# Attention scores of four heads side by side in 32-row tiles instead of stacked key rows

## The reference

```python
q = (query @ Wq.T).reshape(B, L, H, D) * scale      # L = 256, H = 16, D = 32
k = (key @ Wk.T).reshape(B, -1, H, D)               # key = value = ctx_1024, 25088 x 512
v = (value @ Wv.T).reshape(B, -1, H, D)
scores = jax.nn.sigmoid(jnp.einsum('blhd,bshd->bhls', q, k))
o = jnp.einsum('bhls,bshd->blhd', scores, v).reshape(B, L, E)
return o @ Wo.T
```

## Time and profile before

| | us |
|---|---|
| median of three executions | 2024.05 |
| the profiled execution | 2024.77 |
| its span, first to last instruction | 2023.1 |
| TensorE matmul busy | 1986.1 (98%) |
| TensorE weight load busy | 1777.9 (88%) |
| VectorE busy | 1225.8 (61%) |
| ScalarE busy | 1006.7 (50%) |

### The profile page before, as it was taken

One profiled execution on the slowest core, in us unless ns is written; L12 is line 12 of the kernel. 1 busy time (PEld: TensorE's weight loads), 2 busy tenths in 40 slices (PEclk: granted clock), 3 DMA queues, 4 the chain that ended last, 5 costly groups with the idle time before them and its releaser, 6 DMA issues. The chain is left out here.

```text
span 2023.1 us, 50717 instructions
## 1 busy us (share of the span) xinstructions
PE 1986.1 (98%) x19340; PEld 1777.9 (88%) x19340; DVE 1225.8 (61%) x2116; ACT 1006.7 (50%) x1129; POOL 26.8 (1%) x31
## 2 busy tenths in 40 slices
PE   7999999999999999999999999999999999988999
PEld 6888999888899988889998888999888899756998
DVE  6666566666656666665666666566666656335322
ACT  3445555454555545455554545555454555533764
POOL 4000000000000000000000000000000000000000
PEclk9999999999999999999999999999999999999999
DMA  5555655555565555556555555555555554543784
GB/s 189 132 155 151 161 136 153 144 143 150 150 161 136 153 144 143 150 150 161 136 154 143 143 150 150 161 136 153 144 143 150 150 151 107 132 160 127 270 286 160
DMA packets 127938, 311.95 MB, mean 154 GB/s; under 512 B 33720, under 2 KB 33720, under 8 KB 108856
## 3 DMA queue, kind: packets, MB, share of 16 engines
q1 hardware_dynamic: 95784, 215.93, 41.1%
q10 hardware_dynamic: 32112, 95.43, 15.0%
HBM read 155.52 MB, written 1.57 MB: 78 GB/s over the span
## 5 line engine op out<-in xcount | busy, mean ns | idle before, releaser
L346 ACT ACTIVATE probs<-sc 128x1024 f32<-128x1024 f32 x784 | 760.7, 1023 | 793.2 <-PE sc L647 786.7
L613 PE MATMUL kp<-x_combos,weights_r 128*128 128x256 f32 x4116 | 552.7, 284 | 8.2 <-DVE x_combos L448 3.5
L613 PEld LDWEIGHTS kp<-x_combos,weights_r 128*128 128x128 f32 x4116 | 521.1, 193 | 9.1 <-DVE x_combos L448 3.7
L632 PE MATMUL vp<-more_weights,x_combos 128*128 128x256 f32 x3528 | 472.7, 284 | 3.6 <-DVE v L497 3.6
L647 PE MATMUL sc<-rows_r,k_stack_r 96*128 96x256 f32 x3136 | 452.2, 287 | 2.8 <-ACT probs L346 2.8
L632 PEld LDWEIGHTS vp<-more_weights,x_combos 128*128 128x128 f32 x3528 | 446.1, 193 | 3.7 <-issue 3.7
L647 PEld LDWEIGHTS sc<-rows_r,k_stack_r 96*128 96x128 f32 x3136 | 404.0, 192 | 45.2 <-issue 40.7
L662 PE MATMUL acc<-probs,v 128*32 128x256 f32 x6272 | 360.6, 382 | 0.1
L476 DVE TENSOR_TENSOR k_parts<-k_parts,kp 128x512 f32<-128x512 f32 x245 | 168.2, 687 | 306.7 <-PE kp L613 306.7
L662 PEld LDWEIGHTS acc<-probs,v 128*32 128x32 f32 x6272 | 194.3, 110 | 131.7 <-issue 1.4
L448 DVE TENSOR_TENSOR x_combos<-ctx_raw,x_combos 128x512 fp32r<-128x512 f32 x240 | 169.2, 705 | 8.1
(11 more groups left out here) (145 smaller groups left out, 958.3 us busy)
## 6 DMA issues: line engine op xcount, KB each, us to landing
k_stack_r<-k_rows_hi SPq DMA_DIRECT2D x784, 64.0 KB, 2.3
k_stack_r<-k_rows_lo SPq DMA_DIRECT2D x784, 64.0 KB, 2.0
k_stack_r<-k_stack_r SPq DMA_DIRECT2D x196, 256.0 KB, 3.0
ctx_raw<-ctxT_dram ACTq DMA_DIRECT2D x47, 1024.0 KB, 5.7
piece<-w_all_dram ACTq DMA_DIRECT2D x176, 256.0 KB, 5.0
w_raw<-w_all_dram SPq DMA_DIRECT2D x44, 1024.0 KB, 4.8
weights<-wqk_dram SPq DMA_DIRECT2D x2, 1024.0 KB, 11.6
rows_r<-q_rows SPq DMA_DIRECT2D x3, 512.0 KB, 7.6
```

The source lines that it names most:

```text
L346: nc.scalar.activation(probs[:, t % 2, g, :], sc[g % 2][:], ACT.Sigmoid).then_inc(probs_ready, 1)
L613: last = nc.tensor.matmul(k2[:, r, :], wk[i - 1][:, k, a, r * P:(r + 1) * P], xc[:, i - 1, k, b, :], start=i in FRESH and n == 0, stop=n = ...
L632: last = nc.tensor.matmul(v2[:, r, :], xc[:, i - 1, k, b, r * P:(r + 1) * P], wv_c[i - 1][:, k, a, :], start=i in FRESH and n == 0, stop=n ...
```

## The change

The stacks, `stack_rows` and all key DMAs go. The projected rows are written to `k_rows`, which has two parities (chunks) of four quadrants, hi and lo. `scores` now reads them where they lie: head j has partitions 32j to 32j + 31, so each matmul uses 32 rows of the array, and the four heads of a group use four different row strips. The three terms hi·hi, hi·lo, lo·hi, once done by stacking, are now three accumulating matmuls. A call makes two groups: 2 groups × 3 terms × 4 heads = 24 matmuls of 32 rows × 128 columns against 256 query columns, where 8 matmuls of 96 rows stood. Each head writes to its own PSUM bank, so the score tile `sc_heads` takes the place of both `sc` tiles: it holds two groups, and there is one of it. One sigmoid reads all of it (2048 elements a partition, once instead of twice 1024), and the next pair waits for that sigmoid. The order of pairs over tiles and groups changes with it. The loads of the context and of the scanned pieces move from ScalarE's queue to SyncE's. The queries need no stack either; at the start their two trips through memory go. In TensorE's written order, K4 and V4 are parted, and V4 to V7 and P3 to P7 trade places:
P0 K1 V1 P1 K2 V2 P2 K3 V3 K4 P3 W01 P4 V4 K5 P5 V5 K6 P6 V6 K7 V7 P7 W23.

```diff
-        kst, kst_f32 = keep["two_types"](stack, "k_stack", [P, 2, 2, HG, 2, HS])
+        k_rows, k_rows_f32 = keep["two_types"](stack, "k_rows", [P, 2, 4, 2, 2, HS])
-        kr_hi, kr_lo = sb("k_rows_hi", [P, 2, 2, HS], F32R), sb("k_rows_lo", [P, 2, 2, HS], F32R)
-        sc = [stack.enter_context(nc.psum_tensor(f"sc{i}", [P, HG * L], F32)) for i in range(2)]
+        sc_heads = stack.enter_context(nc.psum_tensor("sc", [P, HG, 2, L], F32))
...
+        BY_HALF = [(t, g) for half, groups in enumerate(((0, 2), (2, 0))) for g in groups for t in (2 * half, 2 * half + 1)]
+        BY_TILE = [(t, g) for t in range(TC) for g in (0, 2)]
+        PAIRS = len(BY_HALF)
+        AT_HALF = {(0, 0): 0, (0, 2): 1, (1, 2): 2, (1, 0): 3}
...
-            for q in range(4):
-                stack_rows(0, q)
...
             def sigmoid(c, n, at, first):
...
-                nc.scalar.activation(probs[:, t % 2, g, :], sc[g % 2][:], ACT.Sigmoid).then_inc(probs_ready, 1)
+                nc.scalar.activation(probs[:, t % 2, g:g + 2, :].rearrange("p h (j l) -> p h j l", j=HG),
+                                     sc_heads[:, :, :, :].rearrange("p j h l -> p h j l"),
+                                     ACT.Sigmoid).then_inc(probs_ready, 1)
...
                 if i >= 5:
                     dve.wait_ge(k_sum, m * 5 + (i - 2))
-                    at = q % 2
-                    if q == 2:
-                        dve.wait_ge(hi_moved[0], m * MOVED + MOVED)
-                        dve.wait_ge(lo_moved[0], m * MOVED + MOVED)
...
-                    nc.vector.tensor_copy(kr_hi[:, at, :, :], to).then_inc(k_hi, 1)
+                    nc.vector.tensor_copy(k_rows[:, par, q, 0, :, :], to).then_inc(k_hi, 1)
...
-            def scores(c, n, order, free):
+            def scores(c, par, n, order, free):
                 t, g = order[n]
+                half = t // 2
                 if free:
-                    pe.wait_ge(probs_ready, c * (TC * G) + (n - 1))
...
-                for j in range(HG):
-                    last = nc.tensor.matmul(sc[g % 2][:, j * L:(j + 1) * L],
-                                            kst[0:3 * D, t // 2, g // 2, j, g % 2, t % 2 * P:(t % 2 + 1) * P],
-                                            qst[0:3 * D, j, g, :], start=True, stop=True)
+                    pe.wait_ge(probs_ready, c * PAIRS + n)
+                q = AT_HALF[half, g]
+                if q == 0:
+                    pe.wait_ge(k11_lo, c + 1)
+                else:
+                    pe.wait_ge(k_lo, c * 3 + q)
+                for r in range(2):
+                    for k_part, q_part in ((0, 0), (0, 1), (1, 0)):
+                        for j in range(HG):
+                            rows = slice(D * j, D * (j + 1))
+                            last = nc.tensor.matmul(sc_heads[:, j, r, :],
+                                                    k_rows[rows, par, q, k_part, r, t % 2 * P:(t % 2 + 1) * P],
+                                                    q_rows[q_part][rows, g + r, :], start=(k_part, q_part) == (0, 0),
+                                                    stop=k_part == 1)
                 last.then_inc(scores_ready, 1)
...
                 pair(2)
                 keys(3)
                 v_product(m, 3)
+                keys(4)
                 pair(3)
-                keys(4)
-                v_product(m, 4)
                 weigh(c, par, 0, BY_HALF)
                 weigh(c, par, 1, BY_HALF)
                 pair(4)
+                v_product(m, 4)
                 keys(5)
+                pair(5)
                 v_product(m, 5)
-                pair(5)
                 keys(6)
+                pair(6)
                 v_product(m, 6)
-                pair(6)
                 keys(7)
+                v_product(m, 7)
                 pair(7)
-                v_product(m, 7)
                 weigh(c, par, 2, BY_HALF)
```

More of the change, by code:

```diff
@@ L269, in _, with scan_piece @@
-            sp.dma_start(f32(qst[2 * D:3 * D, :, :, :]), kept_q[1]).then_inc(q_stacked, 16)
-            for q in range(4):
-                stack_rows(0, q)
             sp.dma_start(x1[:], x_rows).then_inc(x_loaded, 16)
             def one(c, par, first, k_next, split_next, looped):
[L274 to L278, removed]
+                def scan_piece(t):
+                    sp.wait_ge(piece_used, c * TC + (t - t % 2 - TC + 1))
+                    sp.dma_start(piece[:, t % 2, :], w_all[c - 1][:, t * PIECE:(t + 1) * PIECE].bitcast(I32)
+                                 ).then_inc(piece_loaded[t % 2], 16)
@@ L280, in _ @@
+                if looped:
+                    scan_piece(0)
+                    scan_piece(1)
+                if split_next:
+                    sp.wait_ge(x_ready, c * 7 + 14)
+                    sp.dma_start(raw[:], ctxT[c + 2]).then_inc(ctx_loaded, 16)
+                if looped:
+                    scan_piece(2)
+                    scan_piece(3)
             chunks(sp, one)
@@ L390, in _ @@
                 elif i == 4:
-                    k_first(0, first=True)
+                    k_first(0, 0)
                     v_first(0, 0)
@@ L464, in wk_rest, with k_first_rest, k_summed @@
                                         f32(wk[i - 1][:, :, 0, :]), ALU.subtract).then_inc(wk_ready, 1)
-            def k_first_rest(m, first=False):
+            def k_first_rest(m, par):
                 dve.wait_ge(k11_hi, m + 1)
-                if not first:
-                    dve.wait_ge(lo_moved[2], m * MOVED)
-                nc.vector.tensor_tensor(kr_lo[:, 0, :, :], k2, f32(kr_hi[:, 0, :, :]), ALU.subtract).then_inc(k11_lo, 1)
-            def k_summed(m, i, first=False):
+                nc.vector.tensor_tensor(k_rows[:, par, 0, 1, :, :], k2, f32(k_rows[:, par, 0, 0, :, :]),
+                                        ALU.subtract).then_inc(k11_lo, 1)
+            def k_summed(m, par, i):
                 add, q = SUMS[i]
@@ L657, in weigh @@
                     pe.wait_ge(v_sum, c * 5 + 5)
-                for n, g in ((n, g) for n, (tile, g) in enumerate(order) if tile == t):
-                    pe.wait_ge(probs_ready, c * (TC * G) + (n + 1))
+                for n, g in ((n, g + r) for n, (tile, g) in enumerate(order) if tile == t for r in range(2)):
+                    pe.wait_ge(probs_ready, c * PAIRS + (n + 1))
                     for j in range(HG):
@@ L678, in pair @@
                 def pair(p):
-                    for n in (2 * p, 2 * p + 1):
-                        scores(c, n, BY_HALF if k_next else BY_TILE, not (first and p == 0))
+                    scores(c, par, p, BY_HALF if k_next else BY_TILE, not (first and p == 0))
                 def keys(i):
```

82 lines of the change are left out of this document (24 added, 58 removed).

## The result

The changed kernel takes 2460.89 us in the median of four executions (2457.36 to 2464.48), against 2024.12 for the kernel before: ratio 1.216, 95% interval 1.214 to 1.218. It is 437 us slower. The forecast was 2275, with a range up to 2335. The sign was right; the size was off by 186 us.

What follows compares the result with a forecast made beforehand. The prediction took TensorE's own program as the bound. Its sum: 2024.8 + 189 + 9 (chunks 0, 45, 46) + 0.6 (chunk 47) + 59 (clock) - 10 (start) + 3 (end) = 2275 us, range 2200 to 2335.

Steps and rivals of the forecast that it cites:

- Step 1: Score block on TensorE: 24 matmuls on four strips take 0.76 us where 0.96 stood, -1.6 us a chunk.
- Step 2: Mode changes around TensorE's score blocks: 0.18 us each, +2.2 us a chunk.
- Step 3: TensorE waits 3.7 us at K6 in each looped chunk for VectorE's read of K5: +189 us over 44 chunks.
- Step 4: TensorE's clock falls after each K6 wait, costing 1.3 us in a looped chunk: +59 us in all.
- Step 5: Kernel's start without key DMA waits: -10 us; last chunk with a single score tile: +3 us.
- Step 6: Key DMAs, the loop's sigmoids and SyncE's queue: costed at nothing.

Runs made afterwards that it cites:

- e3: Changed kernel with VectorE's combinations ahead of V4's sum and TensorE's 44 looped chunks written out without a loop: 2037.92 us, ratio 1.007 to the kernel before.
- e9: e1 with its loop kept, but score blocks leave out the lo-keys term, 16 matmuls instead of 24: 2068.17 us, ratio 1.022 to the kernel before.
- e7: e2 with TensorE's blocks in the whole order of the kernel before: 2080.11 us.
- e6: e2 with V4 moved back ahead of the weighing in TensorE's order, only K6 between P5 and P6: 2063.94 us.
- e5: e2 with 15 matmuls of zeros ahead of K6, keeping TensorE busy through the wait: 2214.42 us, ratio 1.094 to the kernel before.
- e1: Changed kernel, loop kept, with VectorE's three combinations and first two scans ahead of V4's sum: 2212.89 us, ratio 1.093 to the kernel before.
- e11: e2 with V4 ahead of the weighing and a K and a V product ahead of each pair from P5 on: 2038.75 us.
- e2: Changed kernel with TensorE's 44 looped chunks written out, other engines' loops kept: 2279.61 us, ratio 1.126 to the kernel before.
- e4: Kernel before, with four chunks instead of two in TensorE's loop body: 2098.71 us, ratio 1.037 to the kernel before.
- e8: e3 with a score block's loops of terms and heads exchanged, so three matmuls in a row use one 32-row strip: 2042.7 us.
- e12: e3 with heads outermost in a score block, so all six matmuls of a head follow each other: 2448.6 us.

## Why the prediction was wrong, step by step

- **Step 1, the score block, right.** 0.76 us forecast from first to last start and stagger. Read from e3, 1212.09 to 1213.00 is 0.91 with the change of mode, 0.18: 0.73. Four strips run side by side in fp32r as in f32, at 0.12 a round; e9, with two rounds less, has chunks 1.86 us shorter, 0.116 a round.
- **Step 2, the changes of mode, right.** 0.18 each by the rows before, 0.18 by e7 against e6. Steps 1 and 2 together were to make the chunk 0.6 us longer; it is 0.31 longer. Over 48 chunks the difference is 14 us, the largest error among the terms that stood in the sum.
- **Step 3, the wait at K6, right in place, cause and size.** 3.7 us forecast, 3.47 to 3.6 of idle time in the profile, 3.7 by e5 against e3, and e1 and e11 lift it from either side.
- **Step 4, the clock, right.** 1.3 us for each wait forecast, 1.4 by e5 (1.5 in a looped chunk). The choice of 1.3 over 2.6 leaned on a misread row: in the 8 us before K1 TensorE had done V7 and P0, not one score block alone. That 1.3 came out was in part luck.
- **Step 5, start and end, near.** K1 of chunk 1 starts at 48.78 where the text had 49, but K3 then waits 1.96 us for VectorE's split of the key rows, which the text did not have. The first weighing comes 9.2 us earlier (73.35 to 64.14), for 10 forecast, and the last chunk is some 5 us longer instead of 3.
- **Step 6, what was cost at nothing: here it failed.** Waits, queues and sigmoids were gone through, and the loop was not; the forecast said that no wait but K6's would repeat. Step 1 counts 24 matmuls in place of 8 only by the time that they take in the array. They are also 32 more instructions a block with their weight loads, 256 more in a chunk: the loop body grew from 1440 to 1952 matmuls and weight loads. Between 1440 and 1696 lies a bound above which the body is read anew at every jump back. In the changed kernel TensorE then waits twice, 3.2 and 2.7 us, with a stretch at the lower clock behind: 181 us by e2, and the forecast missed 186. e4 shows the same with the old blocks, so length alone is enough and nothing in the new blocks is needed. The row to watch was on the page of the kernel before: 0.48 MB of instructions for a program whose loop ran 22 times, so its body was read once and kept.

The Trainium skill has a rule on this (Runtime: NRT & Kernel Launch, Instruction fetch mechanics): TensorE's instruction memory holds 2048 instructions and is refilled in blocks of 256, and a taken branch whose target lies outside the current window of two blocks must wait for a fetch. The runs agree on the jump and on the kind of cost. They agree with neither size as a bound for a loop body: bodies of 1767 and 2023 TensorE instructions of all kinds, both under 2048, waited at the jump, and one of 1519, more than five blocks, jumped back with no wait.

The sum with this term would have been 2275 + 181 = 2456, for 2461 measured. That it comes so near is partly luck. The 437 us are 181 at the seam (the changed kernel less e2), 242 at K6 of which 65 clock (e2 less e3, e5), and 14 for the rest (e3). The forecast had nothing for the first, 170 + 59 = 229 for the second, and for the rest 29 - 10 + 3 = 22. So in the sum a K6 that was 13 us too cheap, and a start and end 6 too cheap, stood against blocks and their changes 14 us too dear.

What stays open: how many instructions between 1519 and 1767 may stand in a loop body, why the first wait ends after 3 matmuls and the second does not come in e9, and how TensorE picks among strips (e8, e12).

## What to carry to other kernels

When an edit multiplies instructions inside a hardware loop, count the loop body as well as the array time: the size of the instruction queue's traffic on the page tells whether the body is kept. Here a body a third longer turned a free jump into one of 8.6 us. When two engines keep orders written by hand, moving a block on one of them needs a look at what stands behind it on the other: here V4 moved behind the weighing and P4, and ten unchanged VectorE instructions between its sum and K5's came to hold TensorE up. The same holds for a tile that is now single: with one product instead of two ahead of a pair, TensorE waited for the sigmoid (e6, e7). And splitting the array pays only if the block is long against the two changes of mode around it: here a block of 24 small matmuls took 0.23 us less than the 8 large ones and paid 0.36 for two changes.

## What the runs showed of the hardware that was not expected

- A jump back in TensorE's program cost 5.6 us over 1696 matmuls and weight loads (e9), 8.6 over 1952 (the changed kernel) and 7.5 over 2880 (e4); over 1440 nothing that shows. Straight code of 44 chunks, 3.26 MB of instructions moved, ran without any such wait (e2).
- Six matmuls in a row on one 32-row strip made a block of 24 last 2.02 us instead of 0.98 (e12); three in a row made no difference beyond 0.02 (e8). Each was measured once.
- A wait of 3.6 us filled with 15 zero matmuls kept the granted clock at 1.00 and saved 1.4 us behind it (e5).
- Going from whole-array matmuls to a split of the array, or back, cost 0.18 us (e7 against e6).
